# A vision tower on one Trainium2 core: the order tables written out for every group of images, with five edits beside them

## The reference, cut to what matters

```
h = tokens(x)                      # x: 64 x 12 x 224 x 224 f32, summed over 16 x 16 patches
                                   # -> 64 x 196 x 12, times channel_weights 12 x 192
h = h + attention(layernorm(h))    # one head of 192, softmax over the 196 tokens of an image
h = h + ffn(layernorm(h))          # w_fc * C0, gelu, w_proj * C1; hidden width 768
                                   # C0, C1: masks mixed from alpha_e, alpha_r
```

## Time and profile before

| | before |
|---|---|
| median of the runs | 498.29 us |
| the profiled execution | 498.95 us, span 496.8 us (2.15 us lie around the span) |
| PE, DVE, ACT, POOL busy | 88%, 77%, 57%, 51% of the span |
| TensorE clock granted, mean | 0.935 |
| read, written | 156.29 MB, 9.63 MB |

### The profile page before, as it was taken

One profiled execution on the slowest core, in us unless ns is written; L12 is line 12 of the kernel. 1 busy time (PEld: TensorE's weight loads), 2 busy tenths in 40 slices (PEclk: granted clock), 3 DMA queues, 4 the chain that ended last, 5 costly groups with the idle time before them and its releaser, 6 DMA issues.

```text
span 496.8 us, 11091 instructions
## 1 busy us (share of the span) xinstructions
PE 438.0 (88%) x4654; PEld 370.2 (75%) x4654; DVE 380.4 (77%) x288; ACT 284.7 (57%) x464; POOL 253.6 (51%) x181
## 2 busy tenths in 40 slices
PE   3985445689999999999999999999999999999996
PEld 3653323468787878788878888888888888888986
DVE  1339898998898989898989898989898989510000
ACT  1022021565757575857575757575858585858551
POOL 1014303272747565656565665656565656566570
PEclk9999555558999999999999999999999999999999
DMA  8969999999999999999999999999999998000101
GB/s 246 364 248 323 410 397 403 371 408 379 325 399 405 413 413 412 404 411 405 412 408 408 407 413 405 408 414 412 409 409 406 410 406 347 27 27 26 50 26 48
DMA packets 56661, 166.65 MB, mean 335 GB/s; under 512 B 5972, under 2 KB 13030, under 8 KB 56612
## 3 DMA queue, kind: packets, MB, share of 16 engines
q1 hardware_dynamic: 56612, 165.95, 85.9%
HBM read 156.29 MB, written 9.63 MB: 334 GB/s over the span
## 4 chain that ended last, share of the span: by engine, by line
PE 48%; POOL 23%; issue 12%; ACT 8%; DVE 5%; DMA 3%; SPq 1%; POOLq 0%; ACTq 0%; DVEq 0%
PE ps L522 46%; POOL h_lo L985 10%; POOL inv L964 5%; POOL inv L976 5%; DVE pooled L395 4%; ACT h_hi L894 2%; ACT h_f L885 2%; ACT L885 2%; POOL uhat_tok L978 2%; DMA xs<-x 2%; PE ps L715 1%; POOL phat_tok L969 1%; DMA alpha_sb<-alpha_r 1%; DVE neg_tok L413 0%; ACT out_sb L900 0%
## 5 line engine op out<-in xcount | busy, mean ns | idle before, releaser
L395 DVE TENSOR_REDUCE pooled<-xs 128x28 f32<-128x1792 f32 x144 | 326.3, 2320 | 1.0 <-DMA xs<-x 1.0
L985 POOL TENSOR_TENSOR h_lo<-h_f,h_hi 128x784 fp32r<-128x784 f32 x96 | 176.4, 1868 | 125.8 <-ACT h_hi L894 125.8
L522 PE MATMUL ps<-w_hi,h_hi 128*98 128x192 f32 x768 | 205.2, 267 | 0.0
L522 PE MATMUL ps<-w_lo,h_hi 128*98 128x192 f32 x768 | 194.4, 253 | 0.0
L522 PE MATMUL ps<-w_hi,h_lo 128*98 128x192 f32 x768 | 194.0, 253 | 0.0
L522 PEld LDWEIGHTS ps<-w_hi,h_hi 128*98 128x98 f32 x768 | 126.3, 164 | 18.8 <-issue 15.5
L522 PEld LDWEIGHTS ps<-w_lo,h_hi 128*98 128x98 f32 x768 | 126.7, 165 | 0.0
L522 PEld LDWEIGHTS ps<-w_hi,h_lo 128*98 128x98 f32 x768 | 126.5, 165 | 0.0
L885 ACT ACTIVATE h_f<-ps 128x784 f32<-128x784 f32 x96 | 75.9, 826 | 19.6 <-PE ps L522 19.4
L894 ACT CAST h_hi<-h_f 128x784 fp32r<-128x784 f32 x96 | 81.7, 855 | 0.5
L964 POOL TENSOR_TENSOR inv<-var,minus_half 98x8 f32<-98x8 f32 x16 | 26.2, 1638 | 60.0 <-DVE var L409 60.0
(11 more groups left out here) (119 smaller groups left out, 385.5 us busy)
## 6 DMA issues: line engine op xcount, KB each, us to landing
xs<-x SPq DMA_DIRECT2D x336, 448.0 KB, 7.3
out<-out_sb SPq DMA_DIRECT2D x32, 294.0 KB
rows_sb<-wfc SPq DMA_DIRECT2D x1, 576.0 KB, 6.1
out_sb<-wproj SPq DMA_DIRECT2D x1, 576.0 KB, 9.6
h_f<-wqkv SPq DMA_DIRECT2D x1, 432.0 KB
cf<-const_full SPq DMA_DIRECT2D x1, 264.0 KB, 2.8
h_f<-const_paired SPq DMA_DIRECT2D x1, 153.0 KB, 3.3
cr<-const_rows SPq DMA_DIRECT2D x1, 83.2 KB
```

What stands on the lines that cost most here:

```text
L395: dve.tensor_reduce(pooled[:, n % 2, t, GRID * first:GRID * end].rearrange("p (i j) -> p i j", j=GRID), runs, AX.XY, ALU.add).then_inc(red ...
L522: return pe.matmul(o, a, b, start=start, stop=stop, skip_group_check=shared)
L985: pool.tensor_tensor(h_lo[:, m % 2, t], h_f32[:, t], h_hi[:, m % 2, t].bitcast(F32), ALU.subtract).then_inc(h_lo_ready, 1)
```

## The change

- **Tables by group.** Each unit gets 16 numbers, one for each group; the table covers 4910 steps. The order across groups now differs from group to group. In the middle, the numbers of successive groups grow by 243 to 250 steps instead of 254.
- **Hidden ahead of second scores.** `hidden` of group 0 no longer waits for the exponentials of group 1; `scores` of 1 waits for the gelus of 0, `scores` of 2 for the exponentials of 1, and `hidden` of the last group for the gelus before it.
- **Setup behind the first chain.** `resid`, `f_rows` and `w1` leave `setup()` and are issued at steps of the loop (`SETUP_AT`), in banks 6 and 7. On DVE five chunks of group 0 stand in the setup, in another place.
- **Maxima in the tokens' tile.** DVE writes the maxima into the NEG column of `phat_tok` instead of `neg_tok`; `turn_maxima` is two transposes of `phat_tok` instead of two matmuls of `phat_tok` and two of `neg_tok`. POOL clears the column again in `scale_p` (m >= 2).
- **Table loads.** `load_exp` and `load_gelu`, activations of one element, stand ahead of the exponentials and the gelus.
- `keep_u` waits for the residual of m - 2 (`residual_summed`) instead of its whole output.

```diff
 PERIOD = 254
-STEPS = PERIOD * (GROUPS + 6)
+STEPS = 4910
 PE_ORDER = {
-    "loop": {
-        "hidden": (478, 545, 585),
-        "sum_rows": 58,
-        "scores": 122,
+    "sum_rows": (443, 398, 375, 382, 391, 389, 367, 357, 353, 347, 337, 326, 316, 319, 313, 327),
+    "scores": (545, 646, 525, 534, 526, 522, 511, 505, 501, 491, 481, 470, 451, 444, 461, 430),
+    "hidden": (
+        (799, 936, 890, 888, 890, 885, 881, 870, 859, 848, 839, 818, 798, 812, 786, 680),
...
 ACT_ORDER = {
-        "take_out": (722, 741, 872, 884),
+    "take_out": (
+        (981, 1151, 1142, 1128, 1104, 1100, 1108, 1098, 1087, 1076, 1071, 1050, 1018, 1038, 996, 900),
+        (991, 1156, 1150, 1148, 1129, 1125, 1128, 1117, 1106, 1096, 1076, 1070, 1034, 1043, 1000, 916),
...
 DVE_ORDER = {
-        "reduce": (48, 84, 106, 156, 173, 195, 221, 244, 278),
+    "reduce": (
+        (101, 162, 142, 115, 126, 119, 111, 104, 96, 88, 81, 74, 68, 60, 56, 57),
+        (124, 182, 167, 135, 147, 139, 131, 124, 116, 108, 101, 94, 88, 80, 76, 79),
...
 SP_ORDER = {
-        "load": (173, 186, 224, 243, 263, 321, 324, 359, 393),
-        "send": (1257, 1431),
+        (214, 275, 255, 228, 240, 232, 224, 217, 209, 201, 194, 187, 181, 173, 169, 170),
+        (237, 295, 280, 248, 260, 252, 244, 237, 229, 221, 214, 207, 201, 193, 189, 192),
...
+    "send": (
+        (1089, 1254, 1247, 1246, 1226, 1223, 1225, 1215, 1204, 1194, 1174, 1168, 1131, 1140, 1098, 1014),
...
+SETUP_AT = {
+    "pe_resid": 335, "pe_f": (389, 416), "pe_w1": (457, 494),
+    "act_f": 447, "act_w1": (476, 505), "dve_resid": 383,
+    "pool_wproj": 385, "pool_w1": 517,
 }
...
                 dve.tensor_reduce(
-                    neg_tok[:, :, 2 * pair:2 * pair + 2, NEG].rearrange("p h b -> p b h"),
+                    phat_tok[:, m % 2, :, 2 * pair:2 * pair + 2, NEG].rearrange("p h b -> p b h"),
...
             setup_centre()
+            setup_gram()
             setup_mix()
-            setup_gram()
             reduce_chunk(0, 0)
+            reduce_chunk(0, 1)
             setup_scores()
+            reduce_chunk(0, 2)
             setup_basis()
-            reduce_chunk(0, 1)
+            reduce_chunk(0, 3)
+            reduce_chunk(0, 4)
+            setup_bias()
             setup_g2()
-            setup_bias()
-            reduce_chunk(0, 2)
-            setup_resid()
-            reduce_chunk(0, 3)
...
+            def setup_resid():
                 pe.wait_ge(setup_dve, DVE_BIAS)
-                o = ps[:, 5, 0:EMBED]
+                pe.wait_ge(setup_act, ACT_W0T)
+                o = ps[:, 7, 0:EMBED]
...
-                if m >= 2:
+
+                if m == 1:
+                    pe.wait_ge(gelu_done, HT)
+                elif m == 2:
+                    pe.wait_ge(probs_ready, 4)
+                elif m:
                     pe.wait_ge(gelu_done, HT * (m - 1))
...
-                else:
-
-                    pe.wait_ge(setup_dve, DVE_RESID)
-                for h in range(2):
-                    mm(ps[:, MB, HALF * h:HALF * (h + 1)], phat_tok[:, m % 2, h].rearrange("p b r -> p (b r)"),
-                       ident[0:HALF, 0:HALF], h == 0, False, shared=True)
                 pe.wait_ge(max_ready, 2 * m + 2)
                 for h in range(2):
-                    last = mm(ps[:, MB, HALF * h:HALF * (h + 1)], neg_tok[:, h].rearrange("p b r -> p (b r)"),
-                              ident[0:HALF, 0:HALF], False, h == 1, shared=True)
+                    last = pe.transpose(ps[:, MB, HALF * h:HALF * (h + 1)],
+                                        phat_tok[:, m % 2, h].rearrange("p b r -> p (b r)"), ident[0:HALF, 0:HALF])
...
-                    if m + 1 < GROUPS:
+                    if m == 0:
+                        pe.wait_ge(setup_act, ACT_F)
+                    elif m + 1 < GROUPS:
 
                         pe.wait_ge(probs_ready, 2 * (m + 1) + 2)
+                    else:
+                        pe.wait_ge(gelu_done, HT * m)
...
+            def load_exp(m):
+
+                if m == 0:
+                    act.wait_ge(cleared, CLEARED)
+                act.activation(table_out[:], minus_half[0:1, 0:1], ACT.Exp)
+
+            def load_gelu(m):
+                act.activation(table_out[:], minus_half[0:1, 0:1], ACT.Gelu_apprx_tanh)
...
-                    act.wait_ge(out_summed, 4 * (m - 1))
+
+                    act.wait_ge(residual_summed, 2 * (m - 1))
...
                 if m >= 2:
 
                     pool.wait_ge(context_summed, m - 1)
+                    pool.memset(phat_tok[:, m % 2, :, :, NEG:NEG + 1], 0.0).then_inc(neg_cleared, 1)
+                    pool.wait_ge(neg_cleared, m - 1)
```

More of the change, by code:

```diff
@@ L70 @@
 PERIOD = 254
-STEPS = PERIOD * (GROUPS + 6)
+STEPS = 4910
 PE_ORDER = {
-    "loop": {
[L74 to L77, removed]
-        "hidden": (478, 545, 585),
-        "apply_g2": 296,
-        "sum_rows": 58,
-        "turn_phat": 91,
-        "apply_a": 120,
-        "turn_uhat": 375,
-        "scores": 122,
[L85 to L89, removed]
+    "sum_rows": (443, 398, 375, 382, 391, 389, 367, 357, 353, 347, 337, 326, 316, 319, 313, 327),
+    "turn_phat": (518, 448, 469, 453, 465, 487, 469, 462, 459, 448, 438, 427, 388, 397, 400, 390),
+    "apply_a": (531, 461, 487, 472, 504, 503, 487, 481, 477, 467, 457, 446, 405, 420, 419, 408),
+    "scores": (545, 646, 525, 534, 526, 522, 511, 505, 501, 491, 481, 470, 451, 444, 461, 430),
+    "turn_maxima": (582, 684, 626, 582, 574, 576, 576, 565, 555, 545, 534, 524, 504, 498, 506, 470),
+    "turned_scores": (596, 698, 642, 596, 589, 591, 591, 588, 571, 560, 549, 539, 519, 513, 521, 486),
+    "weigh": (627, 732, 673, 627, 625, 627, 623, 619, 607, 597, 586, 576, 555, 553, 567, 524),
+    "turn_context": (645, 755, 692, 651, 649, 655, 649, 645, 635, 625, 614, 603, 579, 581, 607, 550),
+    "turn_u": (705, 798, 723, 680, 681, 704, 698, 695, 684, 674, 663, 656, 616, 619, 626, 569),
+    "apply_g2": (720, 813, 772, 709, 720, 726, 720, 716, 706, 695, 684, 680, 641, 679, 647, 603),
+    "residual": (
+        (724, 850, 1043, 1039, 1028, 1022, 1018, 1008, 998, 987, 972, 961, 939, 930, 903, 838),
+        (1000, 1163, 1159, 1155, 1149, 1145, 1134, 1124, 1113, 1103, 1089, 1080, 1040, 1050, 1007, 923),
+    ),
+    "turn_uhat": (784, 865, 821, 798, 799, 810, 799, 790, 779, 752, 747, 738, 716, 735, 704, 645),
+    "hidden": (
[3 rows of a table added]
+    ),
+    "project": (
[24 rows of a table added]
+    ),
@@ L90 @@
 }
 ACT_ORDER = {
[L92 to L97, removed]
-        "take_out": (722, 741, 872, 884),
[L99 to L105, removed]
+    "load_exp": (360, 648, 478, 532, 505, 501, 514, 508, 504, 494, 484, 473, 462, 447, 437, 445),
@@ new lines @@
+    "load_gelu": (625, 925, 879, 873, 879, 879, 876, 859, 848, 837, 827, 802, 801, 805, 769, 677),
+    "copy_context": (640, 745, 686, 640, 638, 647, 643, 639, 627, 617, 606, 595, 573, 575, 598, 539),
+    "copy_u": (713, 806, 759, 688, 707, 716, 710, 706, 696, 686, 675, 667, 628, 637, 642, 578),
+    "keep_u": (717, 810, 801, 692, 718, 727, 721, 718, 707, 697, 686, 682, 639, 648, 685, 582),
+    "copy_uhat": (792, 873, 828, 805, 807, 818, 807, 797, 787, 761, 755, 746, 724, 743, 714, 656),
+    "gelu": (
[6 rows of a table added]
+    ),
@@ L106 @@
+    "round_high": (
[6 rows of a table added]
+    ),
+    "take_out": (
[4 rows of a table added]
+    ),
 }
 DVE_ORDER = {
-    "loop": {
-        "context": 526,
-        "reduce": (48, 84, 106, 156, 173, 195, 221, 244, 278),
[L111 to L114, removed]
+    "reduce": (
[9 rows of a table added]
+    ),
+    "variance1": (486, 416, 428, 421, 413, 440, 398, 420, 412, 404, 368, 362, 354, 355, 358, 346),
+    "maxima": (
+        (561, 663, 538, 558, 550, 543, 535, 527, 520, 512, 507, 499, 475, 476, 477, 443),
+        (571, 673, 548, 568, 560, 552, 545, 537, 529, 522, 517, 509, 484, 485, 486, 453),
+    ),
@@ L293, in build @@
         h_lo_ready = sem("h_lo_ready")
+        residual_summed = sem("residual_summed")
         out_summed = sem("out_summed")
@@ L505, in _ @@
                     for c in range(PER_GROUP):
-                        if now == at["reduce"][c] and (m > 0 or c >= 4):
+                        if now == at["reduce"][c] and (m > 0 or c >= 5):
                             reduce_chunk(m, c)
@@ L599, in setup, with setup_f, setup_w1 @@
                 mm(o, cr[0:1, ROW_ONE_U:ROW_ONE_U + 128], bproj_sb[0:1, :], False, True).then_inc(setup_pe, 1)
+            def setup_f(j):
                 pe.wait_ge(setup_pool, POOL_W0T_1)
                 pe.wait_ge(setup_act, ACT_W0T)
[L603 to L607, removed]
+                pe.wait_ge(setup_dve, DVE_RESID)
+                o = ps[:, 6 + j, 0:384]
+                mm(o, basis_t[:, 0, :], w0t[:, 0, 384 * j:384 * (j + 1)], True, False)
+                mm(o, basis_t[0:E2, 1, :], w0t[0:E2, 1, 384 * j:384 * (j + 1)], False, True).then_inc(setup_pe, 1)
+            def setup_w1(part):
```

(43 more changed lines are left out.)

62 lines of the change are left out of this document (41 added, 21 removed), and 60 rows, old and new, of tables (ACT_ORDER, DVE_ORDER, PE_ORDER, POOL_ORDER).

## The result

The changed kernel takes 493.21 us (median of 16 runs, 492.44 to 496.9), the kernel before 498.33 in the same rounds: ratio 0.9909, 95% interval 0.9894 to 0.9924. The forecast was 485 us; the gain is 5 us where 13 were forecast. The time lies in the range and next to rival B (492), but rival B's mechanism is not what the profile shows. The profiled execution took 494.9 us (span 492.8), 1.7 us above the median; its rows are read with that in mind.

The account below looks back on a forecast made before the run. Transfers were taken as the bound, 25.2 us per group. Last `sum_rows` 430.1 - 13 + 1 - 4 = 414.1, plus 66.7 and 2.8 gives span 483.6; with 2.15 around it, less 0.66 for the median, 485.1; range 476 to 494.

Parts of the forecast that it names:

- rival B: Front: only the hole of 30 to 50 us is refilled, PE's slow clock delays early groups, stock unused; 492 us, chance 0.17.
- Part 5: ACT's own table loads, the relaxed `keep_u` wait and PE's moved setup: chains don't end the middle, so 0.
- Part 1: DVE's setup order and the tables' front: fills the 30 to 50 us hole and removes a send stall; -13 us.
- Part 2: Middle groups: tighter tables cannot beat transfers at 25.2 us per group, +1 us; the landed data shrinks, -4 us.
- stock: Landed x data that DVE has not yet summed: shrinks from 7.6 us to about 3.5, worth -4 us.
- Part 3: Hidden of group 0 ahead of scores of 1: outputs ready earlier for SP's sends, by itself worth 0 at the end.
- Part 4: Maxima in the tokens' tile: PE saves 0.57 us per group, hidden behind transfers in the middle; only the last group's counts.
- PE's surplus: PE needs about 23.2 us per group against the transfers' 25.2: 2 us to spare, 24 us over 12 groups.
- Part 6: The end: the new PE order leaves more projections and hidden work after the last `sum_rows`; +2.8 us.
- A: The forecast itself: transfers bind throughout and the front is refilled; 480 to 489 us, 485 expected, chance 0.58.
- C: Middle: transfers have room, so groups shrink to 24.1 to 24.4 us; 479 us, down to 473; chance 0.15.
- D: SP's queue: sends waiting for late copies block the loads, once per group; slower, 519 us, chance 0.05.

Follow-up runs that it names:

- the good place: Changed kernel with only `table_out` allocated behind all other tiles, so `xs` begins at byte 49920 instead of 49952: 481.23 us, ratio 0.9665 to the kernel before.
- bare stream: Kernel with all computation left out, only reading x and writing a cleared output: 407 GB/s with `xs` at 16512 or 16544, 418 at 49920; no time given.

## Why the prediction was wrong, point by point

**What failed.** Part 5 costed the own table loads by ScalarE's time alone, at 0. The tile that they write moved `xs` by 32 bytes, and that costs 493.21 - 481.23 = 12.0 us. That `table_out` is new and stands ahead of `xs` could be seen in the two kernels, and I didn't ask what is allocated behind it. In the sum the 12 us sit in the rates: I took 416 GB/s for reads and 25.2 us per group, and got 403 and 25.6. With `table_out` elsewhere the same change takes 481.2 us, 3.8 us under my sum. In its profiled execution the last `sum_rows` starts 2.9 us ahead of the forecast (411.23 for 414.1) and the tail is 1.4 us shorter (68.1 for 69.5).

**Part 1, the front (-13): right in mechanism, less came of it at the result's rate.** The fifth chunk is summed by 28.3 us (26.23 + 2.02 in DVE's timeline), the hole is filled, the first send goes out at 103.66 instead of 121.41 without a hole behind it, and the stretch 30 to 150 moves 403 GB/s. Against the 416 that I took for the ceiling this loses 120 x (1 - 403/416) = 3.8 us. In the good place it moved 416 to the end. The setup order alone brings 5 us.

**Part 2, spacing (+1) and stock (-4).** That transfers and not the tables set the spacing of the changed kernel was right. That they already did so in the kernel before was not: its 10.24 MB per 25.1 us are 408 GB/s by what the engines asked for, DVE never waits for x in its middle, and transfers are 3% of its chain. The size wasn't right either: I took 25.2 us per group from a growing landing time. With a full queue in the good place it is 10.24/0.412 = 24.8 us, in the other 25.6. The row on which I refused room, 0.08 us more landing time per group, did not show a limit at 408 GB/s. For the changed kernel 11 groups at 25.6 instead of 25.2 are 4.4 us. The stock shrank as forecast: the last run is issued at 407.1, lands 12.4 us later at 419.5, and the last chunk is summed at 423.0, 3.5 us behind (3.5 forecast, 7.6 before).

**The error of 10.6 us in the last `sum_rows`** (424.67 for 414.1) by these rows: 4.4 us from the middle, some 2 from the front (3.8 less the 1.7 that I had left out), 1.2 because the first 30 us moved 308 GB/s instead of 324 (30 x 16/416), and 1.2 because PE comes to `sum_rows` 1.7 us behind the last chunk instead of 0.5. That is 8.8 us; the other 1.8 is not placed. The profiled execution lay 1.7 us above the median, where I had reckoned with 0.66.

**Part 3 (0)** was not tried alone, and neither were the new tables. In the good place the whole change gains 17 us; the setup order alone gains 5, and undoing the maxima or the table loads costs 2.7 and 5. What is left, some 4 us if the parts simply add up, belongs to them together, and that they add up is not shown. **Part 4:** I had 0.6 us for the whole kernel; undone, it costs 2.2 to 2.7. The last `sum_rows` waits 1.9 us behind its last chunk there (412.94 after 411.06) against 0.8 in the run with both (411.23 after 410.46). So PE's surplus was smaller than I made it. **Part 5:** besides the place, the loads themselves bring 4.5 to 5 us, not 0: "Chains aren't what ends the middle" left out the first groups and the last. **Part 6 (+2.8):** the tail took 68.1 us instead of 66.7, half of it.

**The rivals.** A's picture (transfers bind throughout) is what the profile shows. B's number was hit without its mechanism, by luck: the front was refilled and the stock used, and the slower place took the gain back. In the good place the kernel stands between A and C, to which I gave 0.15: 481.2 us, with 24.8 us per group against A's 25.2 and C's 24.1 to 24.4, and with DVE still waiting for x, which C had not. D did not appear: the transfers are busy without a pause up to 400 us. The 425 GB/s of the Trainium skill (DMA: Bandwidth & Descriptors, section Bandwidth, Measured), which I had weighed against 408, was not reached. The page took it with transfers issued from GpSimd, these are issued from SyncE; 418 is the most in the stretches given here.

## What to carry to other kernels

When a kernel is bound by transfers, the start address of the destination is part of its tuning: look at what a new tile, however small, moves, and put small tiles behind large ones. A rate read while the engines set the pace is no ceiling, even where the DMA share is above 1 (1.03 at 408 GB/s here), and a slowly growing landing time is no measure of one; a stream alone in the same place, or a version of the kernel that waits for its data, is. Test the parts of a bundle one by one in the version that is freed of its accidental cost: here one part seemed to give all of the gain, while with the others the same kernel in the good place gains 12 us more, which the shift took back.

## What the runs showed of the hardware

- Reads of 3584 bytes for each partition ran at 418 GB/s into a tile that begins at a multiple of 256 bytes (49920, 50176), at 403 to 407 GB/s into one 32, 64, 128 or 160 bytes beyond (the last two in a bare stream only).
- With 6, 8 or up to 14 runs of 448 KB in flight the changed kernel's rate is the same within 1% (398, 399, 400 GB/s); only the landing time changes (7.5 to 12.7 us). A bare stream reached 407 at 14 in flight, 406 at 7 and 355 at 4; with one write for each 10 reads 407, 408 and 361.
